# The second attention's opening: key passes placed ahead of and between the transposes of the norm

## The reference, cut to what matters

```python
x = x + _L1_xattn_ref(_layernorm(x, axis=-1), ctx_4096, L1_xattn_Wq, L1_xattn_Wk, L1_xattn_Wv, L1_xattn_Wo)

def _L1_xattn_ref(latents, context, Wq, Wk, Wv, Wo):
    H, KV, HD = (16, 4, 96)
    hidden = jnp.concatenate([context, latents], axis=1)      # 1601 rows of context, then 64 latents
    q = (latents @ Wq.T).reshape(b, q_len, H, HD)
    k = (hidden @ Wk.T).reshape(b, s_len, KV, HD)
    v = (hidden @ Wv.T).reshape(b, s_len, KV, HD)
    ...
    attn = jax.nn.softmax(scores.astype(jnp.float32), axis=-1).astype(q.dtype)
    out = jnp.einsum('bkgqs,bksd->bkgqd', attn, v)
    ...
    return out @ Wo.T
```

## Time and profile before

| | |
|---|---|
| median of three timed runs | 3865.53 us |
| profiled execution, its own time | 3856.49 us |
| its span | 3854.8 us |
| TensorE matmul busy over the span | 94% |
| VectorE, ScalarE, GpSimd busy | 58%, 42%, 33% |
| mean granted TensorE clock | 0.963 of 2.4 GHz |

### The profile page before, as it was taken

One profiled execution on the slowest core, in us unless ns is written; L12 is line 12 of the kernel. 1 busy time (PEld: TensorE's weight loads), 2 busy tenths in 40 slices (PEclk: granted clock), 3 DMA queues, 4 the chain that ended last, 5 costly groups with the idle time before them and its releaser, 6 DMA issues. The chain is left out here.

```text
span 3854.8 us, 75904 instructions
## 1 busy us (share of the span) xinstructions
PE 3619.2 (94%) x32856; PEld 2526.8 (66%) x32856; DVE 2254.2 (58%) x2469; ACT 1607.5 (42%) x2213; POOL 1281.2 (33%) x792
## 2 busy tenths in 40 slices
PE   7999999999779779999999999999999998797998
PEld 4555556555345555788888888888888846454554
DVE  4666666666369852555555555555555515697972
ACT  2555555555269421222222222222222103697950
POOL 4344344342048520222222222222221004285861
PEclk8999999999789889999999999999999999898999
DMA  6455555553111032111111111111111112111110
GB/s 209 126 136 148 141 140 147 141 138 103 41 55 52 12 142 80 29 42 41 49 41 49 41 41 50 41 49 41 49 41 45 72 42 55 41 51 31 52 45 22
DMA packets 215252, 277.14 MB, mean 72 GB/s; under 512 B 67056, under 2 KB 165328, under 8 KB 213632
## 3 DMA queue, kind: packets, MB, share of 16 engines
q1 hardware_dynamic: 214920, 272.28, 24.3%
HBM read 218.63 MB, written 53.13 MB: 70 GB/s over the span
## 5 line engine op out<-in xcount | busy, mean ns | idle before, releaser
L1727 POOL TENSOR_TENSOR D_ctx_lo<-D_ctx_raw,D_ctx_hi 128x2048 fp32r<-128x2048 f32 (+1 forms) x64 | 269.7, 4214 | 1217.8 <-ACT D_ctx_hi L1721 1217.8
L724 DVE TENSOR_REDUCE A_mxc<-A_psX 128x2 f32<-128x768 f32 (+2 forms) x512 | 485.4, 984 | 206.1 <-PE A_psX L754 205.2
L1020 ACT ACTIVATE A_probs<-A_psE 128x1024 f32<-128x1024 f32 (+1 forms) x416 | 426.3, 1025 | 317.3 <-PE A_psE L1053 312.0
L1746 ACT ACTIVATE D_V<-D_psY 128x384 f32<-128x384 f32 x208 | 101.9, 490 | 904.3 <-PE D_psY L1812 904.3
L1762 DVE TENSOR_REDUCE D_mxc<-D_psE 128x4 f32<-128x1536 f32 (+2 forms) x128 | 241.9, 1890 | 235.0 <-PE D_psE L1840 235.0
L2103 ACT ACTIVATE D_probs<-D_psE 128x2048 f32<-128x2048 f32 x112 | 210.4, 1879 | 295.6 <-PE D_psE L2216 295.6
L330 POOL TENSOR_TENSOR ES_hcp<-E_du,E_Cn 128x512 f32<-128x512 f32 x224 | 284.8, 1275 | 128.3 <-DVE E_du L357 97.9
L2232 PE MATMUL D_psO<-D_probs,D_V 128*32 128x256 f32 (+1 forms) x5376 | 313.4, 381 | 0.0
L1802 PE MATMUL D_psY<-D_ctx_hi,D_wk_hi 128*128 128x384 f32 (+2 forms) x768 | 279.9, 364 | 13.4 <-DVE D_K_lo L1757 12.7
L1812 PE MATMUL D_psY<-D_wv_hi,D_ctx_hi 128*128 128x384 f32 x832 | 285.3, 343 | 0.0
L1812 PE MATMUL D_psY<-D_wv_hi,D_ctx_lo 128*128 128x384 f32 x832 | 279.0, 335 | 0.0
(11 more groups left out here) (369 smaller groups left out, 7793.9 us busy)
## 6 DMA issues: line engine op xcount, KB each, us to landing
A_land<-in_ctx SPq DMA_DIRECT2D x32, 768.0 KB, 6.1
D_ctx_raw<-in_ctx SPq DMA_DIRECT2D x32, 768.0 KB, 4.7
A_land<-in_ctx SPq DMA_DIRECT2D x16, 1024.0 KB, 5.7
D_ctx_raw<-in_ctx SPq DMA_DIRECT2D x16, 1024.0 KB, 5.4
E_Cn<-bc_scratch SPq DMA_DIRECT2D x64, 256.0 KB, 3.3
k_scratch<-A_Khl SPq DMA_DIRECT2D x32, 384.0 KB, 5.2
A_Kst<-k_scratch SPq DMA_DIRECT2D x64, 192.0 KB, 3.6
A_land<-in_ctx SPq DMA_DIRECT2D x16, 642.0 KB, 4.4
```

The source lines that it names most:

```text
L724: nc.vector.tensor_reduce(mxc[:, u % 4, :, u // 4], psX[:, x % 2, :, 0:w], axis=AX_X, op=ALU.max).then_inc(x_free, 1)
L1020: nc.scalar.activation(probs[0:KW[k], n % NPR, :, :].rearrange("p h q -> p (h q)"), psE[0:KW[k], :], ACT.Exp, scale=HD ** -0.5).then_inc(e ...
L1727: nc.gpsimd.tensor_tensor(ctx_lo[c][:, :, 0:w], ctx_raw[c][:, :, 0:w], ctx_hi[c][:, :, 0:w].bitcast(F32), ALU.subtract).then_inc(lo_done[c ...
```

## The change

TensorE does the three key passes of chunk 0 first. Then come three rounds of two turns of transposes and one key pass of chunk 1, then the last two turns, and then chunks 2 and 3 as they were. On VectorE two tiles are normalised first, then chunk 0's banks are read, then follow three rounds of two normalisations and one read of a chunk 1 bank. On ScalarE the high part of chunk 1 moves ahead of the eight copies. SyncE and GpSimd keep their lists.

```diff
@@ ScalarE
                     high_part(act, 0, 0)
+                    high_part(act, 0, 1)
                     for t in range(NPAIR):
                         norm.out(act, t)
-                    high_part(act, 0, 1)
                     high_part(act, 0, 2)
@@ VectorE
                     low_weights(0, *wk_parts)
-                    for t in range(NPAIR):
-                        norm.normalise(dve, t)
-                    for c in range(NC):
-                        for t in range(T):
-                            keys_out(dve, link, 0, c, t)
+                    norm.normalise(dve, 0)
+                    norm.normalise(dve, 1)
+                    for t in range(T):
+                        keys_out(dve, link, 0, 0, t)
+                    for t in range(T):
+                        norm.normalise(dve, 2 * t + 2)
+                        norm.normalise(dve, 2 * t + 3)
+                        keys_out(dve, link, 0, 1, t)
+                    for c in range(1, NC):
+                        if c > 1:
+                            for t in range(T):
+                                keys_out(dve, link, 0, c, t)
                         if c == 1:
                             dve.wait_ge(wv_hi, 1)
                             low_weights(1, *wv_parts)
@@ TensorE
-                    for t in range(NPAIR):
+                    def turn(t):
                         if t >= H:
                             pe.wait_ge(norm.t_out, t - H + 1)
                         norm.transposes(pe, t)
+
                     pe.wait_ge(w_split, 1)
-                    for c in range(NC):
+                    for t in range(T):
+                        keys(pe, 0, 0, t)
+                    for t in range(T):
+                        turn(2 * t)
+                        turn(2 * t + 1)
+                        keys(pe, 0, 1, t)
+                    turn(NPAIR - 2)
+                    turn(NPAIR - 1)
+                    for c in range(2, NC):
                         for t in range(T):
                             if c == NC - 1:
                                 pe.wait_ge(made, 1)
```

## The result

The changed kernel takes 3871.14 us, the median of 20 runs (3866.51 to 3875.32), against 3864.2 for 20 runs of the kernel before (3858.32 to 3867.12). The ratio is 1.0018, interval 1.0012 to 1.0025: **slower, by 6.9 us (4.6 to 9.7)**. The profile bears out the direction and most of the mechanism; the timed difference is smaller than the forecast one of 9.2 us.

A forecast was written before the change was run, and what follows sets the result against it. The prediction took the start of the fourth chunk's keys in the second attention's opening as the bound. The latents' later round trip moved it from 1419.01 to 1428.2, +9.2 us on 3865.53: 3874.7 us, range 3871.5 to 3878.5.

The forecast's parts named there:

- The start: Second attention's opening: TensorE starts chunk 0's keys at 1391.27, once the low part is ready, 6.0 us earlier.
- The clock at chunk 0: Chunk 0's first key passes run at half speed for 3.6 to 5.8 us after idling, costing 2.4 us.
- What is late next: Ahead of chunk 2: its high part stands behind all eight copies, so TensorE waits 6.3 us for the low part.
- Chunk 3 hangs on the last transpose: Chunk 3's keys wait for the latents' DRAM round trip after the last turn: 1428.2 against 1419.01, +9.2 us.
- The port: GpSimd's low part of chunk 2 holds the port against VectorE's value-weight split, costing nothing; opposite-way rival +9.6 us, chance 0.03.
- The latents' write: The 2048 KB write to xn_scratch, issued at 1413.0 with nothing beside it, takes 7.1 us instead of 12.8.
- So already before, the fourth chunk hangs on the last transpose: Kernel before: last transpose to chunk 3's keys is a 21.7 us chain through xn_scratch, ending 0.68 us behind TensorE's own work.
- With 1.4 to spare: Chunk 2 ends at 1426.8, 1.4 us before chunk 3 can start; its wait and 2.1 us cold clock are hidden.
- The sum: Whole kernel: +9.2 us on the three-run median 3865.53 gives 3874.7 us, slower by 0.24%.
- The chance of 0.81 for slower by over 0.2%: Whole kernel: forecast 0.70, twice cold or slow write 0.08, and the port going the other way 0.03.
- round trip cheaper: Opening: clock rises sooner or write takes 6.1 us; +5.8 to +7.6 us, within 0.2%; chance 0.13.
- Cold twice: Gap ahead of chunk 3 lowers the clock again, or the write stays slow: +2.1 us or more; chance 0.08.

The follow-up runs named there:

- the warm-up: Changed kernel with 22 identity transposes on TensorE just ahead of chunk 0's keys; ratio to the kernel before 1.0019.
- the experiments on single chains: Changed kernel with chunk 2's high part ahead of the copies (1.0024), or with latent columns loaded from context at the start (1.0017); ratios to the kernel before.
- chunk 2 first: Changed kernel with ScalarE making chunk 2's high part ahead of the eight copies, behind chunk 1's; ratio to the kernel before 1.0024.
- both chains: Changed kernel with chunk 2's high part ahead of the copies and latent columns loaded from context at the start; 3859.84 us, 0.9995 of the kernel before.
- ScalarE's move: Kernel before with only chunk 1's high part moved ahead of ScalarE's copies; ratio to the kernel before 1.0011, +4.2 us.
- the new order with VectorE's subtraction: Kernel before with two turns ahead of chunk 0, six between chunk 1's passes, chunk 3's keys behind the projection, chunk 0's low part on VectorE; 0.9992, repeated 0.9991.
- the first new order: Kernel before with two turns ahead of chunk 0, six between chunk 1's passes, chunk 3's keys behind the projection, chunk 0's low part on GpSimd; 0.9997.
- VectorE's subtraction in the order of before: Kernel before with only chunk 0's low part made by VectorE, between second and third normalisation, instead of GpSimd; ratio to the kernel before 1.0005.

## Why the forecast missed, point by point

**Right.** *The start*: at +14.43 for +13.8; the 0.65 is the first chunk's load, which landed that much later in this execution. *The clock at chunk 0*: priced 2.4, took 2.5 in the trace after and 2.4 when it was taken away by the warm-up. *What is late next*: a wait for chunk 2's low part of 6.3 us, behind ScalarE's last copies; it is 5.97, and the experiment on that chain removed it. *Chunk 3 hangs on the last transpose*, in the changed kernel: it starts +8.7 us, +9.2 forecast. *Afterwards*: in these two profiles it does go to the end. *The port*: GpSimd's low part of chunk 2 (3.42 us, undisturbed) held VectorE's split of the value weights, as the following row of VectorE after shows beside the 1.75 of the earlier trace rows.

```profile
1422.28 3.71 DVE L1959 TENSOR_TENSOR D_wv_lo<-D_wraw,D_wv_hi 128x1536 fp32r<-128x1536 f32 x1 [3.42 <-ACT D_wv_hi L1937]
```

**The latents' write**, a term of the sum: priced at 7.1 from the final store of the same size, it took 6.3, and 6.2 to 6.4 in the eight experiments in which it is issued behind the other transfers. The other row at hand, 6.1 for 1920 KB, was the better guide. This takes 0.8 off; the later start and turns (0.4 us later to the write's issue) give half of it back, and 9.2 becomes 8.7.

**"So already before, the fourth chunk hangs on the last transpose"**: this was misread. The write landed with the end of the DMA traffic, at +33.5, +32.5 and +33.8 when it was issued at +20.7, +23.1 and +18.5. The sum came near because it priced the write anew for the changed kernel and did not carry the old 12.8 over.

**"With 1.4 to spare"**: this failed. The cold clock of chunk 2 was priced at 2.1 and took 9.07 - 6.3 = 2.8; chunk 2 started 0.2 later than forecast; with the cheaper write the latents came 0.5 earlier; and the 1.4 was gone. Chunk 2 does not hide in the shadow of the latents' trip, it ends with it, and the second, shorter wait that the forecast named as a sign is not there. The time is the same either way, but the conclusion "cure the latents' trip and the loss goes" would have been wrong: the experiments on single chains gained nothing.

**The sum** failed at its base, which alone is enough to put the number out of the range. 3865.53 us, the median of three, was taken as if exact. Over 20 runs it is 3864.2, 1.3 lower, with single runs from 3858.32 to 3867.12; three runs within 1.04 us of each other had only looked sharp. The profiled execution at 3856.49, 9.0 below, was on the page and should have been read as that spread. The low end, 3871.5, was worked out as the cheap rival on an exact base; with 1.3 less it would have been 3870.2 and held the result. Of the 3.6 us between forecast and result 1.3 are this base, 0.5 are the opening (the write above all), and 1.8 lie between the trace's +8.7 and the timed +6.9.

**The size itself**: the trace says +8.7 us in the opening and 1.5 more behind it, the timed runs say +6.9 (4.6 to 9.7). The opening's number is inside that interval; that the rest is chance is an argument, not a finding, and the cause of these 1.8 us stays open. For all kernels here the trace's shift at the latents' values agrees with the timed one within 2.2 us; five of them: after +8.7 and +6.9, chunk 2 first +10.1 and +9.3, both chains -0.2 and -1.9, ScalarE's move +3.8 and +4.2, the new order with VectorE's subtraction -5.3 and -3.1.

**The chance of 0.81 for slower by over 0.2%** rested on a centre at 0.24%, 1.5 us above that bound. With a measurement that resolves some 5 us in all, a chance that high was not to be had from 1.5. The rival "round trip cheaper" was right on the write (it assumed 6.1) and wrong on the clock, which rose late (5.3 and 5.9 us), not early. Its verdict, within 0.2%, is the one that was measured, and the time is 0.2 us below its best case; with one of its two reasons gone, that is luck more than a reading. "Cold twice" did not come in this kernel, as no gap is left ahead of chunk 3; where that gap was there, in the first experiment, it did (8.25 us against 6.42).

## What to carry to other kernels

Before work is moved ahead on the engine that bounds, follow what the displaced work releases, its copies and its trips through DRAM above all, to the last consumer: 15 us of delay to eight transposes came back as 8.7 us, although the moved passes themselves started 5.4 earlier. Where two chains end together, mending one shows nothing, so test both at once before a cause is ruled out, and hide the longer one under work that needs neither (here the projection). And read a base's spread from all executions at hand, the profiled one too, before an end of the range is set a microsecond from a bound.

## What the runs showed of the hardware

**The hold is paid again for each subtraction.** When two of GpSimd's subtractions follow each other, each holds a VectorE instruction: with ScalarE's move alone, 4.50 and 3.62 us for pairs of normalisations that take 1.00 undisturbed. In the first new order a pair of normalisations met two subtractions and took 8.10. The same subtraction of 2048 columns takes VectorE 2.28 us and GpSimd 4.5; on GpSimd it held VectorE's pair of the earlier trace rows for 3.9 us, more than VectorE takes to do it. The Trainium skill (SBUF — State Buffer, section "Who interferes with whom") lets whichever engine began first hold the shared port for its whole instruction. The rows agree: VectorE's work ends 0.85 and 0.74 us behind GpSimd's two subtractions with ScalarE's move alone, and the split of the value weights, 1.75 alone, 1.62 behind the one that held it (1425.99 and 1424.37).

**Which gaps lowered the clock.** Idling of 3.06 us ahead of chunk 3 (VectorE's subtraction in the order of before) left the first matmul at 0.41 us, as at full clock; 5.97 and 7.64 us left it at 0.66. Two gaps of 2.98 and 1.70 us with 1.1 us of transposes between them were enough to lower it, though the first alone had left it at 1.00. Back at work it rose after 5.3 and 5.9 us in the profile after.

**What a write costs among loads.** The same 2048 KB took 6.2 to 6.4 us behind the other transfers, 9.4 with ScalarE's move, 12.8 in the kernel before and 15.2 when issued 2.2 us earlier. In these last three it landed 1.1 to 2.1 us after the DMA engines fell idle, at +32.5 to +33.8: an earlier issue brought nothing, and the length from issue to landing told mainly how early it was issued.
